# Loading x1's rows ahead of convolution C's windows on the DMA queue of a fused four-block kernel

## The reference, cut to what matters

```python
x = x + conv3x3(gn(x), w0) + b0                 # A, zero padding
x = x + inverse(gn(x), 5 steps)                 # B, Newton-Schulz, each 128x128 plane a matrix:
                                                #    X = X @ (2I - W @ X), five times
x = x + circular_conv3x3(gn(x), w2)             # C, written with FFTs
x = x + conv3x3(gn(x), K) * mask                # D, zero padding, last row and column masked
```

## Time and profile before

| | |
|---|---|
| median of 3 runs | 736.62 us (734.77 to 741.38) |
| the profiled execution | 734.72 us |
| its span, first to last instruction | 732.6 us |
| PE, DVE, ACT, POOL busy | 83%, 73%, 52%, 27% |
| mean granted TensorE clock | 0.952 of full speed |
| on the chain that ended last | PE 38%, DVE 26%, SP's queue 10%, DMA 8%, ACT 6%, POOL 3% |
| DMA | 76.43 MB, mean 104 GB/s |

### The profile page before, as it was taken

How to read it: one execution, slowest core, us unless ns; L and a number is a source line. 1 busy time by engine, 2 the same in 40 slices (tenths; PEclk the granted TensorE clock), 3 DMA queues, 4 the chain that set the end, 5 groups by cost and what they waited for, 6 DMA issues and landing times.

```text
span 732.6 us, 11297 instructions
## 1 busy us (share of the span) xinstructions
PE 608.0 (83%) x3752; PEld 508.3 (69%) x3752; DVE 534.3 (73%) x1304; ACT 383.9 (52%) x559; POOL 198.3 (27%) x289
## 2 busy tenths in 40 slices
PE   0695679749999989889898989989999969995956
PEld 0464667648777778778776878778777858884644
DVE  3755976656897888797887779886978587648551
ACT  0351347424666556765756456655667436753632
POOL 5132123002252224322331315222333122201302
PEclk9997899969999999999999999999999998999888
DMA  5196001950378332960497234951363135223352
GB/s 152 52 106 183 1 30 34 132 195 30 90 89 259 87 80 57 179 180 29 111 126 215 70 83 70 201 153 43 87 211 81 44 80 166 48 76 73 85 131 57
DMA packets 89124, 76.43 MB, mean 104 GB/s; under 512 B 6572, under 2 KB 81228, under 8 KB 86252
## 3 DMA queue, kind: packets, MB, share of 16 engines
q1 hardware_dynamic: 87548, 74.07, 43.9%
q0 software_dynamic: 1536, 1.86, 1.0%
HBM read 38.14 MB, written 24.25 MB: 85 GB/s over the span
## 4 chain that ended last, share of the span: by engine, by line
PE 38%; DVE 26%; SPq 10%; DMA 8%; issue 8%; ACT 6%; POOL 3%; DVEq 0%; POOLq 0%; ACTq 0%
PE conv_ps L750 21%; DVE zl L1005 5%; DMA x<-x_dram 4%; PE z L831 3%; DMA rows_dram<-x 3%; DVE stB L676 3%; PE z L833 3%; PE z L835 3%; PE z L826 2%; PE z L840 2%; SPq L275 2%; DVE bn_D L538 2%; ACT d_A L650 2%; SPq L377 2%; POOL d_A L623 2%
## 5 line engine op out<-in xcount | busy, mean ns | idle before, releaser
L1005 DVE SCALAR_TENSOR_TENSOR zl<-z,zh 128x1024 fp32r<-128x1024 f32 x128 | 154.5, 1219 | 64.7 <-ACT zh L938 62.3
L831 PE MATMUL z<-zh 128*128 128x256 f32 x512 | 156.5, 306 | 14.9 <-DVE zl L1005 14.9
L938 ACT ACTIVATE zh<-z 128x1024 fp32r<-128x1024 f32 x128 | 130.3, 1019 | 66.9 <-PE z L835 35.5
L833 PE MATMUL z<-zl,zh 128*128 128x256 f32 x512 | 149.1, 291 | 0.0
L835 PE MATMUL z<-zh,zl 128*128 128x256 f32 x512 | 148.7, 290 | 0.0
L831 PEld LDWEIGHTS z<-zh 128*128 128x128 f32 x512 | 102.4, 200 | 23.8 <-DVE zl L1005 20.7
L750 PE MATMUL conv_ps<-d_A,w_D 128*96 128x512 f32 (+1 forms) x432 | 104.2, 390 | 17.5 <-DVE w_D L608 17.1
L750 PE MATMUL conv_ps<-d_C,w_C 128*96 128x512 f32 (+1 forms) x486 | 113.9, 381 | 0.6 <-issue 0.6
L750 PE MATMUL conv_ps<-d_A,w_A 128*96 128x512 f32 (+1 forms) x378 | 93.9, 397 | 14.8 <-DVE w_A L608 10.8
L833 PEld LDWEIGHTS z<-zl,zh 128*128 128x128 f32 x512 | 102.6, 200 | 1.0
L835 PEld LDWEIGHTS z<-zh,zl 128*128 128x128 f32 x512 | 102.4, 200 | 0.0
(11 more groups left out here) (182 smaller groups left out, 890.6 us busy)
## 6 DMA issues: line engine op xcount, KB each, us to landing
x<-x_dram SPq DMA_DIRECT2D x14, 1024.0 KB, 9.1
win_C<-rows_dram SPq DMA_DIRECT2D x40, 256.0 KB, 4.0
rows_dram<-x SPq DMA_DIRECT2D x32, 256.0 KB
win_A<-x SPq DMA_DIRECT2D x48, 160.0 KB
win_D<-out_C SPq DMA_DIRECT2D x7, 1056.0 KB, 6.8
y<-out_D SPq DMA_DIRECT2D x42, 168.0 KB, 3.8
x_dram<-out_A SPq DMA_DIRECT2D x30, 192.0 KB, 2.1
win_D<-out_C SPq DMA_DIRECT2D x14, 160.0 KB, 5.9
```

The lines of the kernel that those rows point to most:

```text
L831: pe.matmul(z[s][:, m, :], zh[s][:, m, 0:128], zh[s][:, m, :], start=False, stop=True, skip_group_check=True)
L833: pe.matmul(z[s][:, m, :], zh[s][:, m, 0:128], zl[s][:, m, :], start=False, stop=True, skip_group_check=True)
L938: act.activation(zh[s][:, :, :], z[s][:, :, :], ACT.Copy, scale=ROOT[j]).then_inc(s_zh[s], 1)
L1005: dve.scalar_tensor_tensor(zl[s][:, :, :], z[s][:, :, :], ROOT[j], zh[s][:, :, :].bitcast(f32), ALU.mult, ALU.subtract).then_inc(s_zl[s], 1)
```

## The change

In `sp_cycle` the call of `load_x1` is moved ahead of the calls of `load_x2`; `keep_x1` of cycle 0 goes with it and stays ahead of `load_x1`.

```diff
         def sp_cycle(sp, i, has_D, has_C, has_A, nxt, load):
-            if has_C:
-                for g in range(NG):
-                    load_x2(sp, i - 1, g)
             if is_int(i, 0):
                 keep_x1(sp, i)
             if nxt:
                 load_x1(sp, i + 1)
+            if has_C:
+                for g in range(NG):
+                    load_x2(sp, i - 1, g)
             if not is_int(i, 0):
                 keep_x1(sp, i)
```

## The result

| | before | changed |
|---|---|---|
| median of 20 runs | 733.19 us (726.0 to 741.55) | 727.24 us (723.72 to 735.45) |
| ratio | | 0.9929, 95% interval 0.9904 to 0.9954 |
| span of the profiled execution | 732.6 us | 725.7 us |
| mean granted TensorE clock | 0.952 | 0.954 |

The changed kernel is 0.7% faster, some 5 us, inside what the text called "within 1%". The forecast was 729.4 us with a gain of 6.2.

A forecast was written before the change was run, and what follows sets the result against it. The load of x1 was taken to bound four cycles through DVE's wait. 1.1 + 0.6 + 2.1 + 1.1 + 2.0 - 0.7 = 6.2 us off 734.72 gives 728.5, plus half of 1.9: 729.4 us, range 724.0 to 736.5.

The forecast's parts named there:

- within 1%: Whole kernel: the measured time stays within 1% of the kernel before, about 7.4 us; chance 0.66.
- x1's landing: SP's queue, cycle 4: x1's load moves 4.9 us earlier, 0.85 us ahead of the windows; DVE's wait falls under 1 us.
- Where it was worth something: DVE's waits for x1 pass 1:1 to TensorE; gains of 0.6, 2.1 and 1.1 us in cycles 3, 4 and 5.
- SP itself pays nothing ... The windows are issued when they were.: SP's queue: one issue of 0.34 us fits into the 0.85 us lead, so C's windows are not issued later.
- The windows' delay, taken as 1.0 us: DMA engines: C's windows land 1.0 us later, bounds 0 and 2.75 us (upper 1.6 in cycle 1).
- Cycle 4 bears 1.3 us of delay: Slot 6 of cycle 4: up to 1.3 us of later windows costs nothing, as DVE is busy with `stB`.
- One sign of being wrong: The forecast is wrong if ACT waits for C's windows by more than 1.3 us in cycles 2 to 5.
- Cycle 1, 1.1 us: Cycle 1: `zl` could start 2.1 us earlier, less 1.0 us for later windows, a gain of 1.1 us.
- the first rival: C's windows land 2.75 us later and take x1's place in the chain; gain 0.9 us, 733.8 us; chance 0.22.
- The clock, 2.0 - 0.7 us: TensorE after L711, cycles 4 and 5: no clock fall gains 2.0 us; possible fall at A's first group costs 0.7.
- The risk of a fall at A's first group in cycle 5: TensorE ahead of A's first group, cycle 5: a clock fall may come, counted as half of 1.5, 0.7 us.
- Rival 2 (slower): x1's load holds back x2's stores and so the windows' issue, 4.0 us late at ACT; 740.0 us; chance 0.06.

The follow-up runs named there:

- e2: Kernel before, with the load of x1 moved ahead of C's windows in cycles 2 to 6 only, cycle 1 as before; ratio 0.9966.
- e3: Kernel before, with x1 loaded twice in cycles 1 to 6, ahead of C's windows and again behind them, DVE waiting for the second; ratio 1.0153.
- e8: The kernel before, unchanged, run once more for a second trace; 733.01 us.
- e7: Changed kernel, but in cycles 1 to 6 ACT issues the load of x1 from its own DMA queue; ratio 0.9971 to the kernel before.
- e10: The changed kernel, run once more for a second trace and ratio; ratio 0.9923 to the kernel before.
- e1: Kernel before, with the load of x1 moved ahead of C's windows in cycle 1 only; ratio 0.9992.
- e4: Changed kernel, with ACT waiting for C's windows group by group instead of for all seven loads; 722.66 us, ratio 0.9893 to the kernel before.
- e6: Changed kernel with ACT's window wait split by group and only x1's first 8 channels loaded ahead of the windows; ratio 0.9869 to the kernel before.

## Why the prediction was right

It called a gain of 6.2 us and 729.4 us; measured were 5 to 6 us and 727.24. The level is partly luck: the 20 runs put the kernel before at 733.19 us, 3.4 under the 736.62 that the forecast started from. The rivals' times were counted from 734.72 us and lack the 0.9 us that the forecast adds. By its own steps:

- **x1's landing.** Right: in cycle 4 it is issued 0.87 us ahead of the first window instead of 4.0 us behind it, 4.9 us earlier, and no wait of DVE for it in any cycle from 1 on.
- **Where it was worth something.** Right for cycles 3 to 5: 0.6, 2.1 and 1.1 were worked out, the idle at L711 fell by 0.65, 1.96 and 1.16. e2 and e3 show that this is cause and not company. But which cycles wait for x1 in the old order is chance (e8), so the terms hold for their sum, not cycle by cycle.
- **"SP itself pays nothing ... The windows are issued when they were."** Wrong. The first one is, the rest is not: six issues take 5.0 us instead of 3.3, on account of the load of x1 ahead, and from another queue too (e7). In cycle 4 this is the whole of the windows' delay.
- **The windows' delay, taken as 1.0 us.** Mis-sized: 1.7 us in cycle 4, within the bounds of 0 and 2.75, and 2.2 in cycle 1, over the 1.6 given there. The idle share of the DMA engines at the windows' start was not filled in full: in the 2 us from 386 to 388 it rose from 0.20 to 0.46, 0.5 us of the 1.6 counted on. The Trainium skill's rule that an engine takes one queue's descriptors in ring order ("DMA: Bandwidth & Descriptors", "Queues, rings and completion order") was taken to mean x1 in full ahead of the windows, 2.75 us in cycle 4 and 1.6 in cycle 1. The measured 1.7 and 2.2 lie under the one and over the other, so that reading fits neither cycle, and e7, with x1 in another queue, has the slower issues too.
- **Cycle 4 bears 1.3 us of delay.** It got 1.7, and `zl` began 0.2 us later than `stB` alone would have let it: right to that. One sign of being wrong did show: ACT waited 1.39 us for the windows there, over the 1.3 named, and 1.57 in cycle 2 of e10. What it cost is small, 0.2 and 0.4 us at L711.
- **Cycle 1, 1.1 us.** Fallen: by the marks 0.1 (means of 15.5 and 15.4 us), and 0.9992 in e1. It is the term that the windows' delay took away. Here the first rival's mechanism holds, in one cycle of five; e4 shows it by removing it.
- **The clock, 2.0 - 0.7 us.** Right in kind and size: two falls after L711 fewer per execution (table), each worth the 1.2 us by which the way to A's first group grew. The risk of a fall at A's first group in cycle 5 was no more than the chance it was called; it came in cycle 3. The changed kernel's two traces have five falls at A in cycles 1 to 5 against four in the two of before, which is of the size of the 0.7 us; over all traces these falls go with nothing, so that this fits is luck.
- **The sum from the four traces** (before and e8 against changed and e10): 0.1 us in cycle 1, 3.3 less of idle at L711 in cycles 2 to 5 where 3.8 were called, and two falls less, 2.3 to 2.4. That is 5.7 to 5.8 us, inside what the ratio's interval leaves (3.4 to 7.0 us). The term that was missing is cycle 1's.
- **Rival 2 (slower)** did not show: the stores of x2 landed 5.5 us after the last was issued in cycle 4, 5.64 before.

The 6.9 us between the two profiled spans is not to be taken as the gain: 1.8 us of it lay ahead of the first difference.

## What to carry to other kernels

When two loads hold up one instruction by two paths, work out the arrival of both before moving one: the one put ahead gains at most until the other is late, and here it gave away in cycle 1 all it had won. Then split the wait of the second (e4): in cycle 1 both edits together brought TensorE forward by 5 us, which neither did alone. A wait of 2 to 3 us ahead of TensorE cost more than itself here, by the 1.2 us of a fall of the clock, so removing half of one can pay for the clock as well.

## What had not been expected of the hardware

- Issuing DMAs from SP slows when a 1 MB load is in flight, even one issued by another engine: SP's six issues of windows took 4.8 to 5.6 us in cycles 1 to 5 of the changed kernel and e10 and in cycle 1 of e1, instead of 3.1 to 3.6 in the two traces of before, one of them 2.05 us alone. With half of x1 ahead they took 4.1 to 5.05 us (e6), and where the load was issued 2 us ahead of the windows, in cycle 6, 4.0 and 4.2 us.
- The same 2.06 us of idle ahead of the same nine matmuls left TensorE at full clock in one cycle (2.32 us) and cost 1.5 us in another (3.87 us), in one execution; which one changed from trace to trace. Ahead of A's first group idle times of 1.74 to 2.30 us went either way; at L711, in cycles 2 to 5, every one from 1.86 us up was followed by a fall, and none up to 1.83 us.
